# A decoder layer with 48 experts: GpSimd's loop of output scatters written out with constant waits, its index copy on VectorE removed

## What is computed

```
logits = where(old_to_new == -1, -inf, layernorm(x) @ gate_weight.T)     # 48 of 128 experts are kept
top_v, top_i = top_k(softmax(logits), 8); top_v /= sum(top_v)
pos = how many earlier (token, expert) choices took this expert          # only pos < 192 is valid
xb[e, pos] = x[token]                                                    # 48 experts x 192 slots
h = silu(xb @ gate.T) * (xb @ up.T)                                      # inner width 192
y = h @ down.T
final[token] += y * weight                                               # a scatter-add of rows of 512
```

## Time and profile before

| what | value |
|---|---|
| three runs | 1112.71 us median, 1108.96 to 1113.69 |
| profiled execution, span from first to last instruction | 1110.6 us |
| busy in the span: PE, DVE, ACT, POOL | 93%, 79%, 57%, 50% |
| granted TensorE clock, mean | 0.981 |
| expert stage, first to last scatter issued | 717.7 to 1101.0 us |

### The profile page before, as it was taken

One profiled execution on the slowest core, in us unless ns is written; L12 is line 12 of the kernel. 1 busy time (PEld: TensorE's weight loads), 2 busy tenths in 40 slices (PEclk: granted clock), 3 DMA queues, 4 the chain that ended last, 5 costly groups with the idle time before them and its releaser, 6 DMA issues.

```text
span 1110.6 us, 24896 instructions
## 1 busy us (share of the span) xinstructions
PE 1032.1 (93%) x6564; PEld 835.1 (75%) x6564; DVE 872.8 (79%) x2430; ACT 628.9 (57%) x1751; POOL 551.0 (50%) x529
## 2 busy tenths in 40 slices
PE   5999899999999999999999977999999999999892
PEld 4777777878878788787887856887777778778781
DVE  5777798888888798888888864677877778787771
ACT  4555445555554554555545441576767767676661
POOL 2124566666666666666666666333433334343333
PEclk9999899999999999999999998999999999999996
DMA  7999574543313122121221210599999999999983
GB/s 287 356 299 288 178 270 161 206 152 138 115 54 96 47 70 72 47 95 47 76 66 49 77 39 20 184 257 246 255 244 246 245 246 256 240 260 241 238 179 46
DMA packets 94051, 185.71 MB, mean 167 GB/s; under 512 B 24791, under 2 KB 24791, under 8 KB 93504
## 3 DMA queue, kind: packets, MB, share of 16 engines
q1 hardware_dynamic: 62640, 145.10, 40.2%
q0 software_dynamic: 31376, 40.20, 17.2%
HBM read 116.00 MB, written 122.00 MB: 214 GB/s over the span
## 4 chain that ended last, share of the span: by engine, by line
PE 26%; DMA 26%; issue 18%; POOL 13%; DVE 10%; ACT 3%; POOLq 1%; DVEq 1%; SPq 0%; ACTq 0%
DMA layer_out<-qk_both,scatter_idx 21%; PE ps L1185 13%; POOL slot_records L544 6%; PE ps L1170 5%; POOL layer_out L625 4%; DVE qk_both L1001 3%; POOL rstd L555 3%; PE ps L1175 2%; PE ps L1316 2%; DMA x_ln<-in_x 2%; PE ps L1212 1%; DVE diff L996 1%; PE ps L1283 1%; DMA slot_records<-row,slot_idx 1%; DMA w_raw<-slot_records 1%
## 5 line engine op out<-in xcount | busy, mean ns | idle before, releaser
L544 POOL DMA_INDIRECT slot_records<-row,slot_idx x256 | 266.1, 1040 | 88.5 <-issue 59.6
L625 POOL DMA_INDIRECT layer_out<-qk_both,scatter_idx x96 | 143.3, 1493 | 256.2 <-DVE scatter_idx L1102 205.3
L555 POOL TENSOR_TENSOR rstd<-mv,neg_half 128x1 f32<-128x1 f32 x96 | 80.0, 833 | 130.2 <-DVE mv L914 78.7
L1185 PE MATMUL ps<-w_high,xn_high 128*128 128x512 f32 x384 | 114.9, 422 | 0.7 <-ACT xn_high L640 0.7
L675 ACT ACTIVATE probs<-ps,neg_max_s 128x128 f32<-128x128 f32 x256 | 90.1, 378 | 33.6 <-DVE neg_max_s L911 33.6
L1341 PE MATMUL ps<-w_high 128*128 128x192 f32 x576 | 90.6, 279 | 19.6 <-DVE w_low L1088 19.2
L1185 PE MATMUL ps<-w_low,xn_high 128*128 128x512 f32 x384 | 108.6, 405 | 0.0
L1185 PE MATMUL ps<-w_high,xn_low 128*128 128x512 f32 x384 | 106.9, 400 | 0.0
L1341 PEld LDWEIGHTS ps<-w_high 128*128 128x128 f32 x576 | 76.0, 191 | 40.0 <-issue 39.3
L640 ACT ACTIVATE xn_t<-ps 128x512 f32<-128x512 f32 x64 | 38.3, 599 | 117.7 <-PE ps L1170 117.7
L1088 DVE TENSOR_TENSOR w_low<-gu_sb,w_high 128x1536 fp32r<-128x1536 f32 x48 | 84.3, 1757 | 7.4 <-ACT w_high L640 4.9
(11 more groups left out here) (165 smaller groups left out, 2462.0 us busy)
## 6 DMA issues: line engine op xcount, KB each, us to landing
gu_sb<-in_gate_up SPq DMA_DIRECT2D x48, 768.0 KB, 5.5
slot_records<-dn_both SPq DMA_DIRECT2D x6, 3366.0 KB, 22.9
w_raw<-slot_records SPq DMA_DIRECT2D x48, 280.5 KB, 4.7
dn_both<-in_down_proj SPq DMA_DIRECT2D x48, 256.0 KB, 3.2
x_ln<-in_x SPq DMA_DIRECT2D x32, 256.0 KB, 2.8
x_res<-in_x SPq DMA_DIRECT2D x32, 256.0 KB, 3.1
ctx_t_sb<-in_ctx_t SPq DMA_DIRECT2D x32, 256.0 KB, 3.6
ctx_sb<-in_ctx_rows SPq DMA_DIRECT2D x32, 256.0 KB, 4.2
```

The source lines that it names most:

```text
L544: pool.indirect_dma_start(out=records, out_offset=bass.IndirectOffsetOnAxis(ap=slot_idx[:, s.parity, k:k + 1], axis=0), in_=row[:, s.parit ...
L555: pool.tensor_tensor(rstd[:, :], mv[:, 1:2], neg_half[:, 0:1], ALU.pow).then_inc(steps.sem, 1)
L625: pool.indirect_dma_start(out=out, out_offset=bass.IndirectOffsetOnAxis(ap=scatter_idx[0:PART[h], d.parity, h:h + 1], axis=0), in_=y[0:PAR ...
L1185: last = pe.matmul(dst, left[:, c, :], right[:, m, c, :], start=(n == 0 and c == 0), stop=(n == 2 and c == KC - 1))
```

## The change

GpSimd no longer runs `expert_turns`. Its 48 experts are written out in a Python loop, so every wait's value is a constant. `settled` is gone. The wait for the adds of the expert before and the wait for y0 stand ahead of the first DMA, the wait for y1 ahead of the second. The DMAs read their row numbers from `slot_table` itself, and the bound is put into a register once. On VectorE the index copy and its semaphore are gone, and the wait for the adds of d - 2 stands ahead of y1 instead of ahead of the index copy.

```diff
@@ gpsimd
-            def expert_turn(b):
-                d = b["down"]
-                if d.exists():
-
-                    if d.back(1).exists():
-                        pool.wait_ge(d_add[d.back(1).parity], moved(d.back(1), 2))
-                    pool.wait_ge(dwn_a.sem, dwn_a.after(d, "y0"))
-                    pool.wait_ge(dwn_v.sem, dwn_v.after(d, "y1"))
-                    pool.wait_ge(dwn_i.sem, dwn_i.after(d, "index"))
-                    settled(pool)
-                    for h in range(2):
-                        pool.indirect_dma_start(
-                            out=out,
-                            out_offset=bass.IndirectOffsetOnAxis(ap=scatter_idx[0:PART[h], d.parity, h:h + 1], axis=0),
-                            in_=y[0:PART[h], d.parity, h, :], in_offset=None,
-                            bounds_check=T + SPARE - 1, oob_is_err=True,
-                            compute_op=ALU.add).then_inc(d_add[d.parity], 16)
-
             for par in range(2):
                 pool.wait_ge(d_x2[par], 16 * NB // 2)
-            expert_turns(pool, expert_turn)
+            last_row = pool.to_reg(T + SPARE - 1)
+
+            def add_outputs(d, h):
+
+                pool.indirect_dma_start(
+                    out=out,
+                    out_offset=bass.IndirectOffsetOnAxis(
+                        ap=slot_table[0:PART[h], 2 * d.index + h:2 * d.index + h + 1], axis=0),
+                    in_=y[0:PART[h], d.parity, h, :], in_offset=None,
+                    bounds_check=last_row, oob_is_err=True,
+                    compute_op=ALU.add).then_inc(d_add[d.parity], 16)
+
+            for e in range(E):
+                d = Batch(e // 2, e % 2, E)
+                if d.back(1).exists():
+                    pool.wait_ge(d_add[d.back(1).parity], moved(d.back(1), 2))
+                pool.wait_ge(dwn_a.sem, dwn_a.after(d, "y0"))
+                add_outputs(d, 0)
+                pool.wait_ge(dwn_v.sem, dwn_v.after(d, "y1"))
+                add_outputs(d, 1)
@@ vector, in the turn, behind gu_low
-                if d.exists():
-                    dve.wait_ge(ffn_w.sem, ffn_w.after(d, "tokens"))
-                    if d.back(2).exists():
-                        dve.wait_ge(d_add[d.back(2).parity], moved(d.back(2), 2))
-                    dve.tensor_scalar_add(scatter_idx[:, d.parity, :],
-                                          slot_table[:, bass.ds(2 * d.index, 2)], 0.0).then_inc(dwn_i.sem, 1)
@@ vector, y1
                     dve.wait_ge(dwn_t.sem, dwn_t.after(d, "y1"))
                     dve.wait_ge(ffn_w.sem, ffn_w.after(d, "weight"))
+                    if d.back(2).exists():
+                        dve.wait_ge(d_add[d.back(2).parity], moved(d.back(2), 2))
                     dve.tensor_scalar(y[0:PART[1], d.parity, 1, :], ps[0:PART[1], 5, :],
                                       weight_of[d.parity][0:PART[1], 1:2], None, ALU.mult).then_inc(dwn_v.sem, 1)
```

More of the change, by code:

```diff
@@ L215, in decoder_layer @@
         slot_table = sb("slot_table", [P, E * 2], I32)
-        scatter_idx = sb("scatter_idx", [P, 2, 2], I32)
         rows = w_raw[:, :, :, :].rearrange("p a c n -> p (a c n)")[:, 0:4 * ROW]\
@@ L324, in decoder_layer @@
         dwn_t = Steps(sem("down_tensor"), "y0 y1")
-        dwn_i = Steps(sem("down_vector_index"), "index")
         dwn_v = Steps(sem("down_vector"), "y1")
```

## The result

The kernel after took 1106.43 us (median of 17 runs, 1104.19 to 1112.41), the kernel before beside it 1113.6 (17 runs): a ratio of 0.9945, 95% interval 0.9929 to 0.9962. A faster kernel had been forecast, but with 1092 us and a range from 1080 to 1102; the gain is about 7 us in place of 20. Executions more than 1.5% above the fastest of their kernel are left out of the ratios.

What follows compares the result with a forecast made beforehand. GpSimd's serial scatter chain, 8.115 us per expert, was taken as the bound. Gains of 18.3 us over 44 periods and 1.65 in the last 3 scatters, together 20, gave a span of 1090.6; forecast 1092 us, range 1080 to 1102.

Steps and rivals of the forecast that it cites:

- The gap: On GpSimd, from a scatter's landing to the next expert's first scatter DMA: 1.02 us was to become 0.33.
- The rival of 0.74: GpSimd takes the DMA up only after its wait: gap 0.74 us, period 7.83, time 1098; chance 0.15.
- The parts costed at nothing: Second DMA's y1 wait, index copy, VectorE's moved wait, row numbers from `slot_table`, written-out code: each taken to change nothing.
- The tail: The last 3 scatters, without loads beside them, were to gain 3 x (0.88 - 0.33) = 1.65 us.
- If the landing stays: Premise that the second scatter DMA still lands after 5.23 us, making GpSimd's chain 7.42 us per expert.
- 44 x (8.115 - 7.70) = 18.3: Gain in us over 44 expert periods, each falling from 8.115 to 7.70 us.
- The loads' +0.2 us: SyncE's rows loads were to land 0.2 us later than 5.6 as the DMA share rises, lengthening TensorE's turn.
- TensorE's 7.34: TensorE's turn per expert without gaps, 7.34 us, read as two turns before any scatter was out.
- The share as a gauge of room: DMA share 0.93 in the expert stage, 1.05 at 20 to 60 us: not capped, but little air.
- DMA engines full: Rival: the share can't pass about 0.95 with scatters among the loads; period 7.95, time 1104; chance 0.10.
- nothing changes: Rival: landings give the cut gap back nearly whole; time 1108 to 1115; chance 0.05.
- The slower rival: Loads fall on the second scatter; a loss past a mean landing of 5.92 us, 1127 at 6.3; chance 0.03.

Runs made afterwards that it cites:

- e1_settled: Kernel after with all waits and `settled` put back ahead of the first scatter DMA; ratio 1.0034 to the kernel before.
- e4_rows_first: Kernel after with SyncE issuing the rows loads ahead of the gate/up load; ratio 0.9939 to the kernel before.
- e6_early_wait: Kernel after with VectorE's wait for the adds of d - 2 back ahead of h1, with `settled`; ratio 0.9939 to the kernel before.
- e10_pitch: Kernel after with slot records of 576 numbers in place of 561, the padding unused; ratio 0.9946 to the kernel before.
- five quarters: Either kernel with one chunk of each expert's gate/up weights loaded a second time; ratios to the kernel before 1.0285 (before) and 1.0345 (after).

## Why the prediction was wrong

**The gap: right.** 0.33 us were taken, 0.29 measured (0.27 in most), in place of 1.07. The rival of 0.74 is out. The rule of the Trainium skill, "Perfetto Trace Analysis", section "DMA Instruction — SWDGE (GPSIMD)", that such a DMA is decoded ahead of its wait, agrees with these 0.27; the one row L535 carried the step.

**The parts costed at nothing: right.** The second DMA's wait for y1 holds GpSimd 2.7 us in all (9 times, up to 0.3). The written-out code shows no fetch stall. The index copy's stall was GpSimd's, not VectorE's own.

**The tail: right.** Three experts without loads were to gain 1.65 us. They gained 2.3 and 1.75 in the two pairs of profiles, and in every kernel that ran the last 3 take 18.3 to 19.4 us with the short gap, 20.7 to 21.0 with the long one (with writes for adds 17.35 and 18.38). The start gave 0.2 to 0.8 where 0 was taken. That makes the ends the one part of the sum that came in as a gain.

**"If the landing stays": the step that failed.** GpSimd's chain of 0.33 + 1.86 + 5.23 = 7.42 took the landing at its old value. It grew by 0.78 on average, all that the gap had released. The sentence ahead of the sum had the premise in it, and the sum didn't price it. With it fell the term 44 x (8.115 - 7.70) = 18.3: the 44 experts took 3.0 us more in one pair of profiles and 1.0 more in the other. `e1_settled` shows the same trade backwards, and with half of the gate/up load the term is there (19.6).

**The loads' +0.2 us: mis-sized.** The mechanism was the right one: TensorE waits for the second rows load, in 24 turns where it had been 5. The landing grew by 0.94 (means 5.55 to 6.49), not by 0.2. The 0.2 came from scaling two stretches with different shares along a line. The share doesn't tell the landing here: 0.93 carried landings of 5.6 in one kernel and of 6.5 in the other.

**TensorE's 7.34: right, from a misread row.** The transposes at 719.68 start 2 us behind the first scatter's issue (717.72), and 712.34 to 719.68 is one turn, not two. The number held: with half loads the period is 7.31.

**The share as a gauge of room.** 0.93 against 1.05 in the first stage was read as "a little air". The share didn't move at all while all landings grew. The rival "DMA engines full" had the loads as its subject, but no cap on the share (7.95 at 0.95) was seen: `e4_rows_first` stands at 0.96 with 8.09, the writes at 0.78 with 7.8. The rival "nothing changes", 1108 to 1115, given back by the landings nearly whole, had the mechanism as measured; it was given 0.05. In size the result lies just below it, by what the ends gained. The slower rival's turning point, a mean landing of 5.92, was a good one: at 5.97 and 5.91 the 44 experts lost 3.0 and 1.0 us. That the whole came out faster all the same lies, in both pairs of profiles, at the ends and ahead of the stage. The page "DMA: Bandwidth & Descriptors" (Trainium skill, section "Latency and other measured facts") sets the memory latency at high load at a multiple of the average one; the prediction used that for the slower rival alone, and the 0.78 us here speak neither for nor against its figure, since the traffic was the same before and after.

**Open.** The steady part of the stage says a loss of 1 to 3 us, the ends a gain of 2 to 3, the medians a gain of 7 (two kernels with the short gap, `e6_early_wait` and `e10_pitch`, gain 1 to 2 us in the steady part too, at the same time as the kernel after, so a few us are what one profile can be off by). In both pairs of profiles 3 to 5 us lie ahead of the expert stage, in code that the change leaves alone; but first transposes start anywhere from 694.7 to 701.0 in kernels with the same first stage (704.3 in the slowest execution with five quarters), 696.3 and 697.7 in two with the old GpSimd loop. Whether some of the 0.55% comes from there wasn't settled. Nor was the mechanism by which a landing grows into the room that it is given, at three quarters of the load and in a turn set by TensorE as well, nor why the expert stage moves 240 to 250 GB/s when the first stage's loads and large stores at 20 to 60 us run at 369: the pitch, the adds against writes and the order were tried, the size of single descriptors and the number of transfers in flight were not. No kernel that ran beat the kernel after with the full computation.

## What to carry to other kernels

Where a serial chain is made of short gaps and a long DMA landing, and the DMA engines have other work beside it, the landing is not a constant: cut the gap only after asking whether another ring through the same engines comes out at the same length. Two rings of equal length with a landing in each were the sign here that a shared resource was between them; less traffic paid (half of one load: 2.5% off the kernel after), a tighter wait didn't. A rate in GB/s at unchanged bytes is the period written another way and proves no limit; vary the bytes. A wait directly ahead of GpSimd's indirect DMA, on a constant, with nothing in between, costs 0.27 us from landing to start in place of 1.02, and pays in stretches where nothing else loads.

## What the runs showed of the hardware

- The landing of the same 64-row scatter-add: 4.26 us with no load beside it, 5.19 in the kernel before, 5.97 in the kernel after, at the same share (0.93) and rate (244 GB/s).
- Turning adds into writes took the DMA share from 0.93 to 0.78 and the period only from 8.10 to 7.81, at the same counted bytes: the share is no gauge of the time that is to be had.
- The landing fills its room at other loads too: the same cut of 0.78 us in the gap lengthened it from 4.87 to 5.62 at three quarters of the gate/up load, 226 to 228 GB/s.
- The second DMA's own time on GpSimd was 1.42 to 2.83 us in the kernel after (over 1.6 in 21 of 48), 1.42 to 1.57 in the kernel before, which has the same loads beside it; why wasn't looked into.
- TensorE's granted clock fell to 1.2 GHz for 3.4 or 6.8 us at a time. In the kernel after it did so four times between the 720th and the 1070th us (17 us); three of these spells begin within 2 us of the end of a standstill of TensorE of 3.4, 1.76 and 1.77 us, and the fourth behind no such one. The kernel before stood still for 1.66 us once and kept 2.4 GHz there. `e4_rows_first` and `e6_early_wait`, with no standstill over 1.5 us, kept it through all 41 experts and took the same time as the kernel after, so the spells cost nothing that could be measured.
